# A graph, mix and feed-forward layer on one core: the edge stage and the closing stage put into one program block, with the closing's loads in 17 parts

## The reference, cut to what matters

```python
xn = layernorm(x)
# graph part: K, Q, V = per-node-type projections of xn
for t in range(ET):
    Ke = einsum('ehd,dk->ehk', K[src], Wa[t]);  Ve = einsum('ehd,dk->ehk', V[src], Wm[t])
    scores = sum(Ke * Q[tgt], -1) * inv_sqrt_dk * relation_pri[t]     # only edges of type t
    w = softmax(scores, axis=0)                                       # over ALL edges of the type
    msgs += where(mask, w[..., None] * Ve, 0.0)
gnn = layernorm(segment_sum(msgs, tgt) + xn) * ln_g + ln_b
mix = linear_attention_block(xn)                                      # one row per node
x = x + gnn + mix
# feed-forward on layernorm(x): the 1561 rows with the largest gate weight get
#   (gelu(row @ w1 + b1) @ w2 + b2) * weight added, all others pass through
```

## Time and profile before

| | |
|---|---|
| time, median of 3 runs | 1071.82 us (1071.51 to 1072.44) |
| the profiled execution: its own time / its span | 1069.83 us / 1068.1 us |
| TensorE busy, share of the span | 880.7 us, 82% |
| VectorE busy | 806.2 us, 75% |
| GpSimd busy | 638.9 us, 60% |
| ScalarE busy | 588.5 us, 55% |
| mean granted clock of TensorE | 0.888 of full speed |
| last edge instruction ends / first closing instruction | 800.6 / 805.9 us |
| first `scale` / last chunk's copy ends | 809.8 / 857.4 us |
| first `up` | 877.8 us |

### The profile page before, as it was taken

How to read it: one execution, slowest core, us unless ns; L and a number is a source line. 1 busy time by engine, 2 the same in 40 slices (tenths; PEclk the granted TensorE clock), 3 DMA queues, 4 the chain that set the end, 5 groups by cost and what they waited for, 6 DMA issues and landing times. The chain is left out here.

```text
span 1068.1 us, 18060 instructions
## 1 busy us (share of the span) xinstructions
PE 880.7 (82%) x5049; PEld 634.7 (59%) x5049; DVE 806.2 (75%) x1708; ACT 588.5 (55%) x1532; POOL 638.9 (60%) x818
## 2 busy tenths in 40 slices
PE   5999999999657877777777777778777948999998
PEld 3776877877434444444444444444447937888886
DVE  6754788888568889898888898988866837886541
ACT  2655999997346666666666666666641213223220
POOL 4615777878677777777777777777720047672000
PEclk9999999999958788888878888887868969999999
DMA  9722344444588888888888888888826332110020
GB/s 284 252 82 90 135 163 146 144 146 153 170 262 252 249 247 250 246 250 254 246 248 254 248 249 252 249 248 252 254 69 242 107 115 70 50 48 4 1 94 27
DMA packets 111497, 189.61 MB, mean 178 GB/s; under 512 B 17861, under 2 KB 80140, under 8 KB 111396
## 3 DMA queue, kind: packets, MB, share of 16 engines
q0 software_dynamic: 38896, 129.86, 39.2%
q1 hardware_dynamic: 69220, 55.29, 16.8%
q10 hardware_dynamic: 3280, 3.28, 0.9%
HBM read 154.21 MB, written 34.16 MB: 176 GB/s over the span
## 5 line engine op out<-in xcount | busy, mean ns | idle before, releaser
L1406 POOL DMA_INDIRECT big<-kv_scratch,src_i x336 | 318.7, 949 | 102.1 <-issue 100.3
L1563 PE MATMUL ps<-edge 64*128 64x256 f32 x784 | 151.3, 519 | 16.2 <-DMA edge<-q_scratch 12.8
L1579 PE MATMUL ps<-big,edge 128*64 128x256 f32 x672 | 118.3, 484 | 37.2 <-DVE big L1748 21.1
L1689 DVE TENSOR_TENSOR big<-big,ps 128x1024 f32<-128x1024 f32 x84 | 102.4, 1219 | 41.0 <-DMA big<-kv_scratch,src_i 37.2
L1563 PEld LDWEIGHTS ps<-edge 64*128 64x128 f32 x784 | 89.5, 246 | 58.2 <-issue 47.7
L1579 PEld LDWEIGHTS ps<-big,edge 128*64 128x64 f32 x672 | 52.7, 167 | 85.5 <-DVE big L1748 43.1
L1477 ACT ACTIVATE edge<-edge 128x64 f32<-128x64 f32 x392 | 102.9, 334 | 0.0
L1696 DVE TENSOR_REDUCE ps<-big 128x32 f32<-128x1024 f32 x84 | 102.5, 1220 | 0.1
L1748 DVE TENSOR_TENSOR big<-big,ps 128x1024 f32<-128x1024 f32 x84 | 99.1, 1213 | 0.0
L2160 ACT ACTIVATE big<-ps,fb 128x256 f32<-128x256 f32 (+2 forms) x104 | 39.5, 462 | 101.9 <-PE ps L2226 101.9
L2226 PE MATMUL ps<-big 128*128 128x256 f32 (+2 forms) x416 | 91.0, 376 | 2.7 <-ACT big L2147 2.7
(11 more groups left out here) (353 smaller groups left out, 1895.8 us busy)
## 6 DMA issues: line engine op xcount, KB each, us to landing
edge<-q_scratch SPq DMA_DIRECT2D x196, 64.0 KB
edge<-key_scratch SPq DMA_DIRECT2D x98, 64.0 KB
big<-kv_scratch,src_i POOLq DMA_INDIRECT x336
agg_scratch<-big SPq DMA_DIRECT2D x16, 252.0 KB
xn_scratch<-big ACTq DMA_DIRECT2D x5, 640.0 KB, 6.6
mix_scratch<-big SPq DMA_DIRECT2D x25, 128.0 KB, 1.7
edge<-mix_scratch SPq DMA_DIRECT2D x1, 3200.0 KB, 12.7
big<-xn_scratch SPq DMA_DIRECT2D x25, 128.0 KB, 2.5
```

The lines of the kernel that those rows point to most:

```text
L1406: pool.indirect_dma_start(kv_slots[s][:, k, :], None, kv_d[0:N, :], bass.IndirectOffsetOnAxis(ap=src_i[:, e:e + 1], axis=0)).then_inc(got[ ...
L1563: ins = pe.matmul(qr_ps[g % 2][:, (2 * hg + k) * D:(2 * hg + k + 1) * D], ohT[64 * hg:64 * hg + 64, g % 2, k * P:(k + 1) * P], qwin[64 * h ...
L1579: ins = pe.matmul(sums_of(g)[64 * hg:64 * hg + 64, :], oneh[:, s, k, hg * 64:hg * 64 + 64], kv_slots[s][:, 2 * hg + k, D:2 * D], start=(k ...
L1689: dve.tensor_tensor(k_rows, k_rows, qr_ps[g % 2].rearrange("p (k d) -> p k d", d=D), ALU.mult).then_inc(pr, 1)
```

## The change

- The closing's functions stand in the same block as the edge stage's, so each engine runs on from one into the other; clear and barrier are gone. GpSimd clears the tables' semaphores after its last fetch and signals `s_fresh`, for which every engine waits once at the start of its closing function.
- The factor steps stand among the last edge groups: the negated maximum behind `subtract` of the last batch, its exponential on ScalarE, the copy of the totals (`zsb`) and the sum by type behind `window_sums(96)`, the five small instructions behind the last `messages`, the six products behind `turn_sums(95)`, the two copies before the last two `keep_sums`.
- Groups 95, 96 and 97 get a PSUM bank and a row buffer of their own, and the order of the last operations on TensorE and ScalarE is new; `spread_maxima(48)` stands ahead of `window_sums(94)`.
- The first waits of the closing stage are on the counts of the edge stage (`ue`).
- SyncE's three loads become 17: 13 parts of the mix rows (256 KB, the last 128 KB), `w1` in two and `w2` in two (512 KB each). Part 0 is issued ahead of the loop, part k+1 behind the store of unit k.
- On GpSimd `root(0, v4, ...)` stands ahead of `gather(3)`.

```diff
 # edge stage, TensorE
                 turn_maxima(NB - 1)
+                spread_maxima(NB - 1)
                 window_sums(NG - 4)
-                spread_maxima(NB - 1)
+                window_sums(NG - 3)
+                totals(NB - 1)
+                window_sums(NG - 2)
+                pe.wait_ge(pd, SELECT_STEPS)
+                pe.wait_ge(s_zk, 1)
+                totals_by_type()
                 turn_sums(NG - 4)
-                window_sums(NG - 3)
-                window_sums(NG - 2)
+                window_sums(NG - 1)
                 turn_sums(NG - 3)
-                totals(NB - 1)
-                window_sums(NG - 1)
+                factors_by_row(1)
                 turn_sums(NG - 2)
                 turn_sums(NG - 1)
...
 # edge stage, ScalarE
+                exponentials(NB - 1)
+                factors_exp(1)
                 keep_rows(NG - 4)
-                exponentials(NB - 1)
+                keep_rows(NG - 3)
+                act.wait_ge(zz, NB)
+                act.activation(zsb[0:4 * TH, :], z_ps, ACT.Copy).then_inc(s_zk, 1)
+                keep_rows(NG - 2)
                 keep_sums(NG - 4)
-                keep_rows(NG - 3)
-                keep_rows(NG - 2)
+                keep_rows(NG - 1)
                 keep_sums(NG - 3)
-                keep_rows(NG - 1)
+                act.wait_ge(yd, FSP_FREE)
+                spread_factors(1, 0)
+                spread_factors(1, 1)
                 keep_sums(NG - 2)
                 keep_sums(NG - 1)
-                act.wait_ge(zz, NB)
-                act.activation(zsb[0:4 * TH, :], z_ps, ACT.Copy).then_inc(s_zk, 1)
...
 # edge stage, VectorE
                 subtract(NB - 1)
+                dve.wait_ge(mr, NB)
+                negate_maximum(c)
                 weights(NB - 1)
                 messages(NG - 2)
                 messages(NG - 1)
-                dve.wait_ge(s_zk, 1)
-                dve.wait_ge(ue, NG)
+                factors(c, 1)
                 n = passes_of(dve)
...
 # edge stage, GpSimd, behind the last fetch
+                pool.wait_ge(yd, NG - RING)
+                pool.sem_clear(range(table_sems[0].num, table_sems[-1].num + 1))
+                pool.sem_inc(s_fresh, 1)
...
-        new_stage()
...
-        with nc.Block() as block:
             @block.sync
             def _(sp):
-                sp.dma_start(rows[:, :, :], mix_d.rearrange("(t p) d -> p t d", p=P)).then_inc(mix_in, 16)
+                sp.wait_ge(s_fresh, 1)
+                sp.wait_ge(s_zrow, 1)
+                sp.wait_ge(ue, NG)
...
-                sp.dma_start(fw1, a["L0_ffn_w1"].rearrange("(c p) f -> p c f", p=P)).then_inc(s_fw, 16)
-                sp.dma_start(fw2, a["L0_ffn_w2"].rearrange("(j p) d -> p j d", p=P)).then_inc(s_fw, 16)
-                sp.wait_ge(s_zrow, 1)
                 sp.dma_start(agg_d[0:1, :], zrow[0:1, :]).then_inc(s_zst, 16)
+                load_part(0)
                 for k in range(NU):
...
+                    load_part(k + 1)
...
 # closing, GpSimd
                 root(1, v3, mv3, rs3, r3)
+                root(0, v4, mv4, rs4, r4)
                 gather(3)
-                root(0, v4, mv4, rs4, r4)
                 gather(4)
...
 # closing, TensorE
-                pe.matmul(ps[0][0:TH, 0:NB], sel96[0:4 * TH, :], zsb[0:4 * TH, :], start=True, stop=True).then_inc(s_fz, 1)
-                pe.wait_ge(s_fac, 1)
...
+                pe.wait_ge(s_fresh, 1)
                 for ck in range(NCK):
+                    if ck < 3:
+                        pe.wait_ge(ue, NG - 2 + ck)
...
 # closing, VectorE
-                c(dve.tensor_reduce(mneg[0:TH, :], mall[0:TH, :], AX, ALU.max))
-                dve.tensor_scalar(mneg[0:TH, :], mneg[0:TH, :], -1.0, None, ALU.mult).then_inc(s_mneg, 1)
...
+                dve.wait_ge(s_fresh, 1)
+                dve.wait_ge(s_zk, 1 + C)
                 dve.memset(zrow, 0.0).then_inc(s_zrow, 1)
                 for k in range(NU):
+                    if k == 0 or (k + 1) * UN > NG - 4:
+                        dve.wait_ge(ue, min(NG, max(NG - 4, (k + 1) * UN)))
```

More of the change, by code:

```diff
@@ L41 @@
 UN, CG = 6, 3
+MIX_PARTS = [(t, min(2, NT - t)) for t in range(0, NT, 2)]
 HP = P // 2
@@ L299, in build @@
         fsp = big.take(C, ETY, NG)
+        FSP_FREE = max(g for g in range(NG) if g % RING == (big.at - 1 - kv_at) // (EG * 2 * D)) + 1
         zrow = big.take(D)
@@ L418, in build @@
         new_stage()
+        s_end, s_fresh = sem("tables_and_mix_stored"), sem("table_semaphores_cleared")
+        g_in, g_kvout, g_qout = (pair(n) for n in ("g_rows", "g_kv_stored", "g_q_stored"))
+        first_of_tables = len(stage_sems)
         vc, pc = sem("vector_step"), sem("pool_step")
@@ L1550, in _ @@
                     act.activation(fb_s3, fb_s3, ACT.Exp).then_inc(fb_n, 1)
+                    factors_exp(2)
+                    for ch in range(C):
+                        spread_factors(2, ch)
             @block.tensor
@@ L1944, in _ @@
                         search(c1, step, 2)
-        new_stage()
[L1949 to L1970, removed]
-        def chunk_groups(ck):
-            return min(CG, NG - ck * CG)
@@ L2005, in build @@
[L2005 to L2014 removed]
+                    negate_maximum(c1)
+                    factors(c1, 2)
+                    dve.wait_ge(s_zk, 1 + 2 * C)
@@ new lines, in build @@
+            assert [s.num for s in table_sems] == list(range(table_sems[0].num, table_sems[-1].num + 1))
+            for s in table_sems:
+                nc.release_semaphore(s)
+            stage_no[0] += 1
+            vc, pc = sem("vector_step"), sem("pool_step")
+            s_zrow, s_zst = sem("zero_row"), sem("zero_row_stored")
+            sc_first, sc_second, ck_ps, ck_kept = (sem(n) for n in (
+                "scaled_first", "scaled_second", "rows_ps", "rows_kept"))
+            ck_st, mix_in = pair("rows_stored"), sem("mix_in")
@@ new lines, in build @@
+            s_fw, s_head, s_tails = sem("ffn_weights_in"), pair("heads_in"), pair("tails_in")
+            s_total, s_totalk, s_totalst = pair("totals_ps"), pair("totals_kept"), sem("totals_stored")
+            ga_in, xn_in = ([sem(f"{n}{k}") for k in range(GR)] for n in ("agg_in", "xn_in"))
+            ad, st3, v3, r3, g1, gs, st4, v4, r4, x3d, rwd, gt = (sem(n) for n in (
+                "with_xn", "gnn_stats", "gnn_var", "gnn_rstd", "gained", "summed", "ffn_stats", "ffn_var", "ffn_rstd",
+                "xf", "row", "gate"))
@@ new lines, in build, with unit_groups, chunk_groups @@
+            x3_T, x3_Tc, h_ps, hd, y_in, y_ok, out_ok, out_st = (sem(n) for n in (
+                "xf_turned", "xf_copied", "h_ps", "h", "y_ps", "y", "out", "out_stored"))
+            s_const3, s_cnt, s_tot, s_eq, s_eqsum, vsel = (sem(n) for n in (
+                "select_constants", "counted", "counts_summed", "equals_marked", "equals_summed", "select_step"))
+            rows, cols = rows_c, cols_c
+            def unit_groups(k):
+                return min(UN, NG - k * UN)
+            def chunk_groups(ck):
+                return min(CG, NG - ck * CG)
@@ new lines, in period, with period_of, place, nodes_in @@
+            def period(p):
+                return range(max(0, GT * p - 1), min(NT, GT * p + GT - 1))
+            def period_of(t):
+                return (t + 1) // GT
+            def place(t):
+                return t - period(period_of(t))[0]
+            def nodes_in(p):
+                return min(N, (period(p)[-1] + 1) * P) - period(p)[0] * P
+            def up_slot(p, q):
+                return q + (p > 0) + sum(NQ + (len(period(r - 1)) if r > 1 else 0) for r in range(p))
+            def y_slot(t):
+                p = period_of(t)
+                return place(t) + (NQ if p == 0 else up_slot(p + 1, NQ if p + 1 < NPER else 0))
@@ L2068, in _ @@
                 c = Chain(pool, pc)
+                pool.wait_ge(s_fresh, 1)
                 pool.wait_ge(s_zst, 16)
@@ L2129, in _ @@
             def _(act):
[L2130 to L2136 removed]
+                act.wait_ge(s_fresh, 1)
                 for ck in range(NCK):
```

131 lines of the change are left out of this document (70 added, 61 removed).

## The result

The changed kernel takes 1062.31 us (median; 1060.05 to 1064.33), the kernel before 1070.63 us beside it: ratio 0.992, 95% interval 0.9903 to 0.9936, or 8.3 us by the medians. The forecast was 6.4 us. Of the 3.1 us down from 1065.4, 1.2 us are the kernel before, whose median was taken as 1071.8 and is 1070.6 here; the other 1.9 us are the change's. The profiled executions differ by 7.5 us in span (1068.1 and 1060.6), and this is the difference that can be followed stage by stage.

The account below looks back on a forecast made before the run. TensorE was taken to bound the kernel, so anything earlier ahead of 877.84 us comes off the end. Terms -7.7 + 1.6 - 0.2 + 0.8 - 0.9 = -6.4 from 1071.8 gave 1065.4 us, range 1061.9 to 1068.5.

Parts of the forecast that it names:

- Start of scaling, -7.7: Edge stage's tail to first `scale`: early factors and no clear or barrier start scaling at 802.1 instead of 809.82, -7.7 us.
- the fetch ends 0.8 us behind the copies: Before scaling: VectorE, fetching instructions after its fallback branch, reaches the closing at 801.9, 0.8 us behind ScalarE's factor copies.
- No second fetch: At the fallback branch: a rival had another instruction fetch in series, 2.8 us more, 1068.2 us; chance 0.16.
- no barrier of 5 us: Hole before scaling: of 5.2 us only 1.7 are clear and barrier, about 3.5 VectorE's way over the fallback.
- The clock, +1.6: Start of scaling: TensorE's clock falls again after its pause; 6.5 us at half pace lose 3.3, against 1.7 before: +1.6.
- the clock doesn't fall: Start of scaling, rival: TensorE's clock stays up after its 1.7 us pause, 3.3 us less, 1062.1 us; chance 0.08.
- The last store, +0.8: End of scaling: part 16 (512 KB), issued just ahead, makes the last small store land 0.8 us later (0 to 1.7).
- The rival of the weight parts slowing four units: Last units of scaling: at 247 GB/s each of four takes 3.1 us, +1.8, 1067.2 us; chance 0.07.
- The pause that went, -0.2: Early scaling: TensorE's 0.2 us pause, from three loads (5.25 MB) ahead of the first store, goes: -0.2 us.
- GpSimd's order, -0.9: After scaling, before `up`: the root ahead of `gather(3)` brings the first transpose 0.9 us sooner (bounds 0 and -1).
- The loads pacing the whole scaling: Scaling, rival: units and parts (9.4 MB) at 170 GB/s take 55 us, giving 1075 us, slower; chance 0.07.
- A wait on `keep`: Scaling: waiting on the ring of two `keep` buffers was named as a sign that the forecast is wrong.

## Why the prediction was right, and where it was not

**Start of scaling, -7.7: right (-7.87), by another last step.** From the last maximum to `scale` the forecast was 12.5 us and the trace has 12.8, where before had 20.2; another 0.5 us is that the last maximum came earlier. `subtract` at 790.45 and the factors' end at 797.75 are each some 0.6 us ahead of the forecast, by about that 0.5. Then the forecast took the clock to be back at 1.00 behind 797.36, as before; here it was at 0.50 until 799.45, `window_sums(97)` took 1.97 us instead of half of it, TensorE starts the factor products at 799.59, and ScalarE's last copy ends at 801.58 instead of 801.1. That is behind the fetch, not ahead of it. The sum did not change, since the two lie some 0.4 us apart. The forecast's picture that the fetch ends 0.8 us behind the copies does not hold in this execution, and there nothing was won without the fallback; it does hold (0.76 to 0.84 us) in the four with the short low stretch and one block.

**No second fetch, and no barrier of 5 us: right.** TensorE's branch took 0.37 us over a longer fallback, and SyncE issued without a pause. Clear and barrier took 1.7 us, as read from the sequencers.

**The clock, +1.6: the wrong size and, in this execution, the wrong sign, -0.4.** It fell behind the pause, as forecast, but for 3.1 us of scaling, where it had been low for 3.4 before. Of the 0.65 us that the products are shorter, 0.2 are the pause that went and 0.4 are left for the clock; the shorter low stretch alone explains 0.15 of these at half pace, and the rest was not followed. With GpSimd's old order, without the fallback and with the split waits, the same stretch was 6.8 us, with the same pause (1.35 to 1.45 us), and cost 2.6 us, not the 3.3 of half pace. So the forecast's 6.5 us nearly occurs, and so does 3.4; the term is one that varies from execution to execution, and one number was too sharp for it. The rival "the clock doesn't fall" named 1062.1, close to the measured time, but not by what happened in this profile: there it fell. It is possible though, as the kernel with the whole loads shows.

**The last store, +0.8: the step that failed, with luck in what hid it.** It cost 2.65 us, more than the bound of 1.7. The forecast fitted store and weight part (764 KB) into a unit's time at 303 GB/s and concluded that nothing piles up, so the last store would wait behind one part at most. The rate was right (260 GB/s at a share of 0.86 is 302 at full share), the conclusion was not: an earlier store of the same buffer took 4.08 us, the last copy had to wait for it, and the last store took 3.71. With the same bytes put first, both were gone. The rival of the weight parts slowing four units had the right transfers and the wrong place: TensorE never waited for them, and only the end did.

**The pause that went, -0.2:** right in sign. But the parts' worth was misjudged: with whole loads the new timing would have lost 3 to 4 us, so that the parts are not a small extra but what lets the early start pay.

**GpSimd's order, -0.9: right** (-0.93 in the profile, undone 1.0). **Behind `up`: nothing was forecast, and 0.7 us came.** The clock rose 3.5 us behind the first `up` instead of 4.9 us, which accounts for it at half pace (1.4 us at half speed is 0.7).

**The loads pacing the whole scaling: refuted.** TensorE is busy for all 30.73 us from 806.27 on, and of the two waits of ScalarE on a store of `keep` (1.0 us at 840.7, where 0.9 is usual, and 1.6 us at the last copy) neither reaches TensorE. A wait on `keep` was named as a sign of being wrong, and the last one is that sign: it belongs to the last store.

The errors had opposite signs: +1.9 at the end, -2.0 by the clock and what is left in scaling, -0.7 behind `up` and -0.2 at the start. They leave -1.1 in the profile, and the difference of the medians is another 0.8 larger. That the total came as near as it did is in part luck: the term for the end and the term for the clock were both wrong by some 2 us, and cancel.

**Left open:** how the 6.6 us that remain with a barrier divide between VectorE's earlier branch, the products' place and the order of the tail; what the kernel gains without the fallback where the low stretch is short; what makes the low stretch in scaling 3.4 or 6.8 us long, or absent, in nearly the same code, and with it whether the transposes prevent it; and why that in the edge stage's tail is 6.8, 10.2, 13.7 or 20.5 us.

## What to carry to other kernels

When a stage is moved forward, ask again what its DMAs meet there: the whole loads had cost 0.2 us at the old timing and 3 to 4 us at the new. Put the largest transfers where nobody waits for a small one behind them; mean bandwidth can fit while the last small store still lands 2 us late. A gap at a block's border is to be split by the sequencers' own rows before it is called a barrier: here it was 1.7 of 5.2 us, the rest the way over a branch, whose cost is hidden only as long as another engine's result is later still. And look at more than one execution before a wait is called covered: here the order in which two waits ended changed from profile to profile, along with the length of a low stretch of the clock.

## What the runs showed of the hardware

- TensorE's granted clock fell to 0.50 around pauses of 1.35 to 2.25 us between busy stretches in five kernels (4.28 us in a sixth, that with the barrier), for 3.4 or 6.8 us. 3.1 us of it in scaling cost 1.1 us of TensorE's time, 6.0 to 6.2 us cost 2.6. It stayed at 1.00 over a pause of 1.81 us in one, and in the three with transposes ahead of a pause of some 1.4 us.
- The low stretch in the edge stage's tail goes with a later end of that stage. In the kernels with one block the last maximum and the first `scale` lie 10.7 to 11.3 us apart where the stretch was 6.8 us long (four kernels), 12.3 to 12.8 us where it was 10.2 or 13.7 (five), and 14.2 us where it was 20.5 (one, which also has the spread later).
- VectorE's way over a fallback that isn't taken is 2.86 to 3.10 us from its branch to its next instruction in nine kernels. TensorE's branch itself took 0.24 to 0.61 us.
- From the last, small store's issue to `tails` it took 1.97 to 2.04 us in the five kernels with nothing large issued just ahead (before, whole loads, weight parts first, and the two built on that), and 3.76 to 4.72 us in the seven in which 512 KB parts go with the last four units.
